# A decoder kernel on one Trainium2 core: one repeated mask product left out of 21 pairs of units in the second self-attention

## What is computed

```python
qkv = hidden_states @ w_qkv.T
q, k, v = jnp.split(qkv, 3, axis=-1)
q = _rms_norm(q, q_norm_w); k = _rms_norm(k, k_norm_w)
# 16 heads of width 16, rotary embedding on q and k
mask = (q_idx >= k_idx) & (q_idx - k_idx <= WINDOW - 1)      # WINDOW = 128
scores = jnp.einsum('bhqd,bhkd->bhqk', q, k) * scale
scores = jnp.where(mask[None, None], scores, -jnp.inf)
probs = jax.nn.softmax(scores, axis=-1)
out = jnp.einsum('bhqk,bhkd->bhqd', probs, v)
```

## Time and profile before

| what | value |
|---|---|
| median of 3 runs | 1411.94 us (1411.03 to 1414.29) |
| the profiled execution | 1419.62 us |
| its span, first to last instruction | 1417.8 us |
| mean granted TensorE clock | 0.929 |
| busy share of the span: PE, DVE, ACT, POOL | 85%, 62%, 39%, 34% |
| chain that ended last: PE, DVE | 66%, 17% |
| first and last mask product (L864) | 594.6 and 683.0 us after the span's start |

### The profile page before, as it was taken

How to read it: one execution, slowest core, us unless ns; L and a number is a source line. 1 busy time by engine, 2 the same in 40 slices (tenths; PEclk the granted TensorE clock), 3 DMA queues, 4 the chain that set the end, 5 groups by cost and what they waited for, 6 DMA issues and landing times.

```text
span 1417.8 us, 21841 instructions
## 1 busy us (share of the span) xinstructions
PE 1202.7 (85%) x7071; PEld 806.6 (57%) x7071; DVE 878.5 (62%) x2229; ACT 557.5 (39%) x1460; POOL 478.3 (34%) x584
## 2 busy tenths in 40 slices
PE   7688998999879959899999989998999409889881
PEld 3554664667744447466774356634667307777770
DVE  1677887753498993766637877587764523444443
ACT  2246776885351101377300167513772302212210
POOL 2253763743100002355400044301442362444444
PEclk9899999999969979899979999999999758999996
DMA  7065996000001001100030000003103523444544
GB/s 293 27 225 171 310 327 191 17 1 1 31 1 44 1 1 75 60 1 2 1 127 1 0 1 1 1 1 131 78 1 119 213 95 69 81 80 81 86 69 108
DMA packets 69612, 110.72 MB, mean 78 GB/s; under 512 B 5056, under 2 KB 59840, under 8 KB 66240
## 3 DMA queue, kind: packets, MB, share of 16 engines
q1 hardware_dynamic: 58896, 96.62, 20.2%
q0 software_dynamic: 10608, 12.72, 5.8%
HBM read 57.41 MB, written 51.91 MB: 77 GB/s over the span
## 4 chain that ended last, share of the span: by engine, by line
PE 66%; DVE 17%; issue 6%; POOL 4%; DMA 3%; ACT 2%; another core or an unknown queue 1%; SPq 1%; POOLq 0%; DVEq 0%; ACTq 0%
PE ps L701 8%; PE ps L690 6%; PE ps L979 6%; PE ps L710 4%; PE ps L682 4%; PE ps L683 3%; PE ps L1033 3%; PE ps L1030 3%; PE ps L960 2%; PE ps L650 2%; PE ps L812 2%; POOL mem L1839 2%; PE ps L864 2%; PE ps L884 2%; PE ps L1049 1%
## 5 line engine op out<-in xcount | busy, mean ns | idle before, releaser
L1839 POOL TENSOR_SCALAR mem<-mem 128x512 f32<-128x512 f32 x256 | 178.4, 701 | 383.9 <-DVE mem L1172 380.6
L1167 DVE TENSOR_REDUCE mem<-ps 128x1 f32<-128x512 f32 x256 | 175.2, 687 | 106.6 <-PE ps L683 98.1
L1665 ACT ACTIVATE mem<-ps,mem 128x512 f32<-128x512 f32 x256 | 177.3, 697 | 13.2 <-DVE mem L1167 12.6
L690 PE MATMUL ps<-mem 128*128 128x128 f32 x1024 | 158.0, 277 | 14.3 <-POOL mem L1839 13.4
L690 PEld LDWEIGHTS ps<-mem 128*128 128x128 f32 x1024 | 117.4, 140 | 69.2 <-POOL mem L1839 51.0
L1658 ACT ACTIVATE mem<-ps 128x512 f32<-128x512 f32 x192 | 116.2, 606 | 90.2 <-PE ps L690 89.7
L1890 POOL DMA_INDIRECT sums<-mem x63 | 97.1, 1542 | 133.1 <-DVE mem L1527 113.5
L682 PE MATMUL ps<-rounded_at 128*128 128x512 f32 x256 | 124.5, 486 | 10.9 <-DVE rounded_at L1156 10.4
L701 PE MATMUL ps<-mem 128*64 128x256 f32 x1024 | 124.6, 385 | 2.4 <-ACT mem L1658 2.4
L1633 ACT ACTIVATE rounded_at<-ps 64x512 fp32r<-64x512 f32 x64 | 37.9, 592 | 165.8 <-PE ps L962 153.0
L683 PE MATMUL ps<-rounded_at 128*128 128x512 f32 x256 | 102.3, 400 | 0.0
(11 more groups left out here) (259 smaller groups left out, 2464.0 us busy)
## 6 DMA issues: line engine op xcount, KB each, us to landing
slots<-mem SPq DMA_DIRECT2D x15, 2312.0 KB, 10.3
mem<-in_f_w_dram SPq DMA_DIRECT2D x16, 1024.0 KB, 9.0
mem<-slots SPq DMA_DIRECT2D x63, 136.0 KB
mem<-in_f_w_dram SPq DMA_DIRECT2D x24, 256.0 KB, 3.3
mem<-in_x_wq_dram SPq DMA_DIRECT2D x2, 2048.0 KB, 13.2
mem<-in_x_wo_dram SPq DMA_DIRECT2D x2, 2048.0 KB, 8.4
mem<-sums SPq DMA_DIRECT2D x8, 256.0 KB, 4.2
mem<-in_x_wqr_dram SPq DMA_DIRECT2D x1, 1536.0 KB, 6.7
```

Of the source, the lines that this page charges most:

```text
L690: mm = pe.transpose(ps[3 + j % 2][:, k * P:(k + 1) * P], PR[j % 6][:, k * P:(k + 1) * P], ident)
L1167: dve.tensor_reduce(nmax[:, i % 8:i % 8 + 1], ps[SB[lay][i % len(SB[lay])]][:, :], AX.X, ALU.max, negate=True)\
L1665: act.activation(PR[i % 6], ps[SB[lay][i % len(SB[lay])]][:, :], ACT.Exp, bias=nmax[:, i % 8:i % 8 + 1], accum_out=esum[:, i % 8:i % 8 + 1 ...
L1839: pool.tensor_scalar(PR[i % 6], PR[i % 6], rinv[:, i % 8:i % 8 + 1], 1.0, ALU.mult, ALU.mult)\
```

## The change

`KEEP` goes from 1 to 0.

```diff
-        KEEP_FIRST, KEEP = 6, 1
+        KEEP_FIRST, KEEP = 6, 0
```

## The result

| | before | after |
|---|---|---|
| median | 1417.26 us (1411.03 to 1424.93, 20 runs) | 1410.72 us (1406.83 to 1418.37, 20 runs) |
| ratio | | 0.9962, 95% interval 0.9944 to 0.9980 |
| the profiled execution | 1419.62 us, span 1417.8 us | 1409.24 us, span 1407.4 us |

The changed kernel is faster, by 0.38% with an interval of 0.20% to 0.56%; that is 5.4 us (2.8 to 7.9) at 1417.26 us. The forecast was 4.5 us. What it missed is the place on the scale. The three runs it started from had a median of 1411.94 us; over 20 runs the same kernel stands at 1417.26. By the ratio, 0.9962 x 1417.26 = 1411.9 us lies 0.6 us above the range of 1404.5 to 1411.3 us; the bare median of the changed kernel's runs, 1410.72 us, lies inside it.

What follows compares the result with a forecast made beforehand. The prediction took PE to bound the stretch from 609.00 to 684.50 us. Removing 21 mask products at 0.215 us each gives 4.5 us, from 1411.94 to 1407.4 us, range 1404.5 to 1411.3 us.

Steps and rivals of the forecast that it cites:

- What bounds the stretch: From 609.00 to 684.50 us PE is busy 75.50 of 75.50 us and bounds the stretch.
- The price of a product: Each mask product removed from pairs 3 to 23 saves the distance between two starts, 0.215 us.
- How many of them are on the path: All 21 products, pairs 3 to 23: pair 3's start stays, each pair passes on 0.215 us, 4.5 us in all.
- What is late next: Transposes waiting for POOL in short turns: slack falls from 0.24 to 0.03 us, costed at nothing.
- The second rival: POOL becomes the bound in seven short turns: gain 3.0 us in place of 4.5, 1408.9 us; chance 0.13.
- The clock: Pairs 3 to 23: 2.4 GHz level holds; rival, it falls to 1.2 GHz, 1472 us if throughout, chance 0.07.
- The gain given back elsewhere: Rival, another part: one more low-clock stretch between parts costs about 1.7 us, leaving 2.8 us, 1409.1 us; chance 0.08.
- The numbers: Whole kernel: 4.5 us off the median of 1411.94 us gives 1407.4 us, 0.32% faster.

Runs made afterwards that it cites:

- the kernel with 129 products: Three repetitions per pair from pair 3 on (KEEP 3), where the kernel before has one: 1424.04 us, ratio to before 1.0062.
- the second time: The changed kernel measured again with no edit, beside the kernel before: 1410.04 us, ratio 0.9972.

## Why the prediction was right in the change and wrong on the scale

**What bounds the stretch.** Right. PE was the chain in all 21 pairs before. After, it is from the middle of pair 3's turn on, at 67.00 of 67.00 us busy.

**The price of a product.** Right. 0.215 us was taken, and the turns after are shorter by 0.21 to 0.22 us wherever the chain is PE; the kernel with 129 products gives the same value in the other direction.

**How many of them are on the path.** One term too many. The prediction said that pair 3's start doesn't move and each pair passes its part on. Of the first two products, pair 3's and pair 4's, only one counted. The turn from pair 3's to pair 4's scores took 3.52 us before and 3.51 after. Before (chain of waits):

```profile
609.78 1.06 PE ps L874 x8
610.85 1.13 PE ps L884 x8
...
613.30 1.06 PE ps L874 x8
```

After (timeline):

```profile
610.95 1.13 PE L874 MATMUL ps<-mem 32*128 32x256 f32 x8
...
614.46 1.13 PE L874 MATMUL ps<-mem 32*128 32x256 f32 x8
```

There POOL's normalisation of pair 1 is what PE waits for (the POOL piece at the head of the new chain), and it starts from ACT's exponentials of pair 1, which the change doesn't move. The sign of it was in the trace before: these eight transposes took 1.13 us where the others take 1.02. The prediction looked for a late POOL in the short turns alone. So 20 products count: 20 x 0.215 = 4.3 us, which is what 76.88 - 72.57 us shows, in place of 4.5.

**What is late next.** Right for the short turns inside the loop, and blind to pair 3's turn, as just said. The slack in a short turn was put at 0.03 us after the change and is 0.02 us. The kernel without mask products shows that it was no more than that: there the chain left PE in the short turns (2.80 to 3.04 us in place of 2.66). The second rival, 1.5 us lost in seven short turns, didn't happen; they read 3.20 us.

**The clock.** Right, and now by more than one stretch. The level held in the changed loop and even without any mask product. The rule of the Trainium skill (TensorE: Matmul & The Clock Gate, Part 4: PE-mode transpose), by which transposes don't count as busy, is not borne out, and the measurement decides: with transposes in place of the early products the clock rose at 606.2 us, behind 5.5 us in which PE had finished nothing but transposes. That is one execution; that transposes count as fully as other products is not shown.

**The gain given back elsewhere.** Partly seen, and the other way: the stretch of low clock behind the stage lasted 20.5 us in both profiles before and 17.1 us in both after. Of the six other profiles, the three with fewer early mask products and the one with three repetitions had 20.5 us again, the one without mask products and the one with early transposes 17.1, so no part of this is claimed for the change.

**The numbers.** This is the step that failed. The prediction took the median of the three runs shown, 1411.94 us, as the kernel's time, and a third of their spread of 3.3 us as its uncertainty (1.1 us, put at 1.2 at the low end; the difference decides nothing). Later runs of the same kernel gave 1417.26 us over 20, 1414.66 over 19 and 1414.96 over 33, and spread over 13 us. Set on 1417.26 us, the same 4.5 us give 1412.8 us; set on 1414.96 us they give 1410.5. The change was off by one product in 21; the value it was taken from was off by more than the whole change. The measured change, 5.4 us (2.8 to 7.9) and the second time 4.0 us (0.4 to 7.4), holds both 4.3 and 4.5 us. Whether anything beyond the loop's 4.3 us is in the first of them stays open: the interval is as wide as the effect, and the turns don't ask for more.

## What to carry to other kernels

Where a loop is PE work without a gap, the distance between two starts times the count gives the gain, and turns read from the chain repeat to a hundredth of a us; judge a change of 0.3% there, and let the timed runs only confirm it. A repetition put in to keep the clock up has to be weighed against the work that is already beside it: here the loop held the 2.4 GHz level by itself. Ahead of the loop, where PE waits, the low level was shorter with six early products (6.8 to 13.7 us) than with none (17 to 24 us), and the products' own time took that back. Before a time is forecast, look at how far single runs of the kernel lie apart in parts that the change doesn't touch: three runs told neither the median nor the spread.

## What the runs showed of the hardware that was not expected

Raising the clock and holding it differ. In the second execution without repetitions PE worked through plain turns without a gap at 1.2 GHz from 603.4 us until the rise just behind 612 us (9.00 of 9.00 us busy from 603 to 612 us). At 2.4 GHz the loop without any mask product, 59.88 of 61.00 us busy, never fell. Why is not shown; at the low level the same instructions also take nearly twice as long (2.08 against 1.13 us for eight score instructions).

And the place of the rise isn't fixed by the program. The same kernel without repetitions rose behind 17 us of the low level in one execution and behind 24 us in another, which moved its stage by 3.0 us (111.3 and 114.3 us): the turn from pair 3's to pair 4's scores took 3.20 us in the one and 5.89 in the other. Six early products gave 13.7 us of the low level in five profiles and 6.8 us in a sixth.
